# Attention's division moved behind the transpose-free layout: numerators, sums and reciprocals carried through DRAM by SyncE

## The chip, the core and the metric

The kernel runs on one core of a Trainium2 chip. The metric is the device time of one execution in microseconds (us); the kernel before takes 2135.75 us (median of three runs). A core has TensorE (PE: matmuls and transposes, called turns here), VectorE (DVE), ScalarE (ACT), GpSimd (POOL), and SyncE (SP), which here issues every DMA. SP takes its instructions in order: while it waits for a semaphore, nothing behind it is issued. The DMAs that it issues go to one queue, served by the core's 16 DMA engines.

## The reference, cut to what matters

A post-norm transformer layer on x of shape (32, 512, 256), with 16 heads of 16 features and a gated FFN of 768 hidden features, all in float32.

```python
qkv = x @ Wqkv
logits = jnp.einsum('bihd,bjhd->bhij', q, k) * scale
logits = logits + SLOPES[None, :, None, None] * rel[None, None, :, :]
logits = jnp.where(causal[None, None, :, :], logits, -jnp.inf)
attn = jax.nn.softmax(logits, axis=-1)
out = jnp.einsum('bhij,bjhd->bihd', attn, v).reshape(Bc, Tc, Dc)
...
x = _layernorm(x + out @ Wout)
gate = jnp.einsum('bsd,hd->bsh', x, wg)
up = jnp.einsum('bsd,hd->bsh', x, wu)
x = _layernorm(x + jnp.einsum('bsh,dh->bsd', silu(gate) * up, wd))
```

The change concerns the division inside the softmax: probabilities are left unnormalised, multiplied with v and a column of ones, and the result is divided by its own sum.

## The kernel before

The work is cut into units: batch b has two units, u = 2b and 2b + 1, of eight heads each; g = 0 or 1 names the group of four heads inside a unit. `Plan` writes one global order of steps, and every engine runs its own steps in that order. The plan goes through windows w. A window has two stages, `attention(w)` and `rest(w)`.

The attention stage interleaves, by the table `ATTENTION`, ten `first` tiles of unit w (PE) each with a `row_max` (DVE), ten `scores` tiles of unit w - 1 (PE) each with an `exp` (ACT) and a `select` (POOL), and three or four pieces of `pv` (PE), each group ending in `pv_copy` (ACT), which puts 128 rows of transposed numerators and sums into `pv_t[g]`: (w-2, 1) in the middle of the stage, (w-1, 0) later in it.

The rest stage has the other matmuls. It differs by part = w % 2. With part 0 (an even window) come `values`, turns of x1 and x, six `gate_up` tiles, `project(w+2, 0)`, `down`, `project(w+2, 1)`. With part 1 (an odd window) come `project(w+2, 0)`, turns of attn, six `gate_up` tiles, two halves of `project_out` (step "out"), `down` and `project(w+2, 1)`. Every `gate_up` tile is followed by `tanh` (ACT) and `silu` (two DVE operations), and `split_h` (`h_hi` on ACT, then `h_lo` on POOL), one tile behind. `down` needs the `split_h` of all six tiles, the last one for its last piece only.

Division before: `turn(u, g)` on PE turns `pv_t[g]` with four 128x128 transposes (L498) into PSUM, where tokens are the partitions. `divide` on DVE takes a reciprocal of the 16 sums (L821) and multiplies (L830) into `attn`. In the odd window PE turns `attn` back with eight transposes; `attn_hi` (ACT, L704) and `attn_lo` (DVE, L786) split it for the `out` matmuls.

SP before, in one window: `spread` (four DMAs of 256 KB, L460, SBUF to the DRAM buffer `bounce`), `gather` (eight DMAs, 1.5 MB, L471, from `bounce` to `q_rows` and `k_rows` of unit w + 1; needed by the first tile `first` of the next attention stage), in even windows `load_residual` and `load_x` (512 KB each, L451 and L444), `store_max` (four DMAs of 8 KB, L480; needed by the first `scores` of the next attention stage), and the output of `norm2` (L485).

## Time and profile before

| | |
|---|---|
| median of three runs | 2135.75 us (2134.16 to 2137.19) |
| the profiled execution | 2136.29 us, its span 2134.6 us |
| PE busy | 93% |
| DVE busy | 75% |
| ACT, POOL busy | 57%, 43% |
| granted TensorE clock, mean | 0.981 |
| DMA queue of SP | 48.5% of 16 engines, 226 MB |
| steady windows 1009.62 to 1040.69 and 1040.69 to 1072.85 | 31.07 and 32.16 us |

A busy share is an average over all stages; matmuls are pipelined, so a busy PE is not at its peak. A time such as 1024.12 is in us from the start of the span. R below is the start of a rest stage on PE: 1024.12 in an odd window and 1055.19 in an even one. An "idle before" or an arrow in a row names what ended the wait.

### The profile page before, as it was taken

What the parts mean: (1) busy time and instruction counts of PE and PEld (TensorE: products, weight loads), DVE (VectorE), ACT (ScalarE), POOL (GpSimd) and SP (SyncE); (2) the same over time, 40 slices, a digit from 0 to 9 for tenths busy, and PEclk for the clock granted to TensorE, in tenths of its full rate; (3) what the DMA queues carried; (4) which work ended last, traced back from release to release, by engine and by line L of the source; (5) the groups of instructions that cost most, each with busy time, mean ns of one, the idle gap of its engine ahead of it and who ended that gap; (6) DMA issues with size and microseconds to landing.
All of it is one profiled execution on the core that took longest, in us unless ns stands there. A gap on an engine that the chain in (4) does not pass through costs nothing.

```text
span 2134.6 us, 47883 instructions
## 1 busy us (share of the span) xinstructions
PE 1983.0 (93%) x19236; PEld 1550.0 (73%) x19236; DVE 1595.1 (75%) x2765; ACT 1223.5 (57%) x1999; POOL 928.5 (43%) x1924
## 2 busy tenths in 40 slices
PE   4779999999999999999999999999999999999986
PEld 3557777777777777777777777777877877777766
DVE  4557777787777787777778777778777778777754
ACT  1446656555655656655655665565565665566552
POOL 0123444444444453444454444444344445444444
PEclk8789999999999999999999999999999999999998
DMA  7455455355555445545545545545554544553500
GB/s 205 103 120 105 101 112 118 96 112 114 115 112 110 103 108 106 128 103 108 113 100 112 121 109 111 116 97 114 106 122 109 106 109 102 111 125 91 100 16 21
DMA packets 148830, 229.09 MB, mean 107 GB/s; under 512 B 13552, under 2 KB 64496, under 8 KB 148592
## 3 DMA queue, kind: packets, MB, share of 16 engines
q1 hardware_dynamic: 148608, 226.02, 48.5%
q8 instruction: 152, 2.49, 0.5%
q14 instruction: 70, 0.57, 0.1%
HBM read 139.98 MB, written 84.93 MB: 105 GB/s over the span
## 4 chain that ended last, share of the span: by engine, by line
PE 80%; DVE 10%; ACT 5%; DMA 2%; issue 1%; SPq 1%; POOL 0%; POOLq 0%; DVEq 0%
PE pair L495 72%; PE pair L498 8%; DVE row_max L801 7%; ACT probs L726 3%; DVE staged_lo L786 2%; ACT staged_hi L704 2%; DMA q_rows<-max_lo 1%; SPq L471 0%; DMA q_rows<-bounce 0%; DMA probs<-L_attn_Wout 0%; SPq L480 0%; DMA bounce<-staged_lo 0%; DVE row_max L803 0%; DVE xt_lo L786 0%; DVE x1t_lo L786 0%
## 5 line engine op out<-in xcount | busy, mean ns | idle before, releaser
L726 ACT ACTIVATE probs<-pair 128x1024 f32<-128x1024 f32 x640 | 627.1, 1027 | 150.1 <-PE pair L495 149.8
L903 POOL TENSOR_SCALAR_AFFINE_SELECT probs<-probs 128x256 f32<-128x256 f32 (+1 forms) x896 | 371.5, 440 | 445.9 <-ACT probs L726 445.1
L910 POOL TENSOR_TENSOR h_lo<-h_full,h_hi 128x256 fp32r<-128x256 f32 x384 | 283.2, 738 | 507.6 <-ACT h_hi L751 496.9
L803 DVE TENSOR_REDUCE row_max<-pair 128x8 f32<-128x1024 f32 x256 | 312.6, 1221 | 115.2 <-PE pair L495 114.7
L801 DVE TENSOR_REDUCE row_max<-pair 128x2 f32<-128x1024 f32 x256 | 311.9, 1218 | 71.2 <-PE pair L495 71.2
L495 PE MATMUL pair<-q_rows,k_rows 64*128 64x512 f32 (+3 forms) x2048 | 321.0, 370 | 38.4 <-DMA q_rows<-max_lo 20.8
L495 PE MATMUL pair<-k_rows,q_rows 52*128 52x512 f32 (+3 forms) x2048 | 299.6, 351 | 60.2 <-DVE staged_lo L786 26.1
L495 PE MATMUL pair<-probs,v_ones 128*32 128x512 f32 (+3 forms) x4096 | 319.3, 441 | 0.8 <-ACT probs L726 0.8
L495 PEld LDWEIGHTS pair<-q_rows,k_rows 64*128 64x128 f32 x2048 | 167.8, 188 | 157.2 <-ACT probs L726 92.2
L495 PEld LDWEIGHTS pair<-k_rows,q_rows 52*128 52x128 f32 x2048 | 179.0, 190 | 122.9 <-DVE row_max L801 62.9
L704 ACT ACTIVATE staged_hi<-pair 128x512 fp32r<-128x512 f32 x128 | 76.6, 599 | 269.9 <-PE pair L495 260.5
L743 ACT ACTIVATE h_full<-pair 128x256 f32<-128x256 f32 x384 | 144.6, 377 | 127.0 <-PE pair L495 126.2
L751 ACT ACTIVATE h_hi<-h_full 128x256 fp32r<-128x256 f32 x384 | 159.6, 416 | 86.4 <-DVE h_full L859 77.7
L495 PEld LDWEIGHTS pair<-probs,v_ones 128*32 128x32 f32 x4096 | 114.3, 110 | 128.5 <-issue 90.5
L495 PE MATMUL pair<-stair,turned 64*128 64x128 bf16 (+1 forms) x2560 | 175.2, 214 | 0.0
L859 DVE SCALAR_TENSOR_TENSOR h_full<-h_full,pair 128x256 f32<-128x256 f32 x384 | 161.7, 421 | 13.2
L734 ACT ACTIVATE pv_t<-pair 128x512 f32<-128x512 f32 x128 | 76.5, 598 | 159.4 <-PE pair L495 159.4
L495 PE MATMUL pair<-x1t_hi,wgate_t 128*128 128x256 f32 x768 | 162.6, 293 | 3.7 <-DVE x1t_lo L786 3.7
L855 DVE SCALAR_TENSOR_TENSOR h_full<-h_full,pair 128x256 f32<-128x256 f32 x384 | 158.2, 412 | 7.3 <-ACT h_full L743 6.1
L495 PE MATMUL pair<-wdown_t,h_hi 128*128 128x256 f32 x768 | 154.8, 283 | 0.6 <-POOL h_lo L910 0.6
L798 DVE TENSOR_REDUCE row_max<-pair 128x4 f32<-128x1024 f32 x128 | 155.4, 1214 | 0.0
L495 PE MATMUL pair<-x1t_hi,wup_t 128*128 128x256 f32 x768 | 155.1, 283 | 0.0
(88 smaller groups left out, 3622.7 us busy)
## 6 DMA issues: line engine op xcount, KB each, us to landing
bounce<-staged_hi SPq DMA_DIRECT2D x128, 256.0 KB
bounce<-staged_lo SPq DMA_DIRECT2D x128, 256.0 KB
q_rows<-bounce SPq DMA_DIRECT2D x128, 256.0 KB, 5.2
k_rows<-bounce SPq DMA_DIRECT2D x128, 256.0 KB, 6.2
x_sb<-L_attn_x SPq DMA_DIRECT2D x32, 512.0 KB, 10.4
k_rows<-bounce SPq DMA_DIRECT2D x128, 128.0 KB, 5.5
q_rows<-bounce SPq DMA_DIRECT2D x128, 128.0 KB, 6.7
x<-L_attn_x SPq DMA_DIRECT2D x32, 512.0 KB, 9.1
```

Source lines behind the costliest of these rows:

```text
L495: return tensor.matmul(o, lhs, rhs, start=start, stop=stop, skip_group_check=True, **kw)
L498: return tensor.transpose(o, i, ident[0:i.shape[0], 0:i.shape[0]])
L726: scalar.activation(probs[g][:, tile, :, :], pair[:, :, :], ACT.Exp, scale=scale).then_inc(s_exp, 1)
L743: scalar.activation(h_full[i % H_BUFFERS][:, :], bank[:, 0:half_tokens], ACT.Tanh, scale=0.5 * W_SCALE).then_inc(s_tanh, 1)
L751: scalar.activation(h_hi[:, m, :], h_full[(n_split_h[step] - 1) % H_BUFFERS][:, :], ACT.Copy).then_inc(s_h_hi, 1)
L798: vector.tensor_reduce(maxima[:, QB1, :, 2 * g:2 * g + 2], pair[:, :, :].rearrange("p s (a n) -> p s a n", a=2), AX.X, ALU.max).then_inc(s ...
L801: vector.tensor_reduce(maxima[:, QB3, :, p], pair[:, :, :], AX.X, ALU.max).then_inc(s_row_max, 1)
L803: vector.tensor_reduce(maxima[:, QB2_PARTS:QB0 + 1, :, p].rearrange("p b s -> p s b"), pair[:, :, :].rearrange("p s (b n) -> p s b n", n=P ...
L855: vector.scalar_tensor_tensor(h_full[z][:, :], h_full[z][:, :], 1.0, bank[:, 0:half_tokens], ALU.add, ALU.mult).then_inc(s_silu_half, 1)
L859: vector.scalar_tensor_tensor(h_full[z][:, :], h_full[z][:, :], 0.5 * W_SCALE * W_SCALE, bank[:, half_tokens:2 * half_tokens], ALU.mult, A ...
L903: made = pool.affine_select(out=diagonal, in_=diagonal, compare_op=ALU.is_ge, fill=0.0, base=0, pattern=[[0, diagonal.shape[1]], [1, P]], ...
L910: pool.tensor_tensor(h_lo[:, m, :], h_full[(n_split_h[step] - 1) % H_BUFFERS][:, :], h_hi[:, m, :].bitcast(F32), ALU.subtract).then_inc(s_ ...
```

## The change

- `turn` and the turns of attn are taken away from PE: 4 transposes for each (u, g), and 8 for each batch. The two-operation `divide` on DVE and `attn_lo` on DVE go with them.
- `send(u, g)`: SP writes `pv_t[g]` (128 rows of 512) to the DRAM buffer `pv_bounce`, after `pv_copy`.
- `fetch(u, g)`: SP waits for the send to land, then issues two DMAs: the numerators (64 rows, read in DRAM as 4 heads x 16 features x 512) into `attn[z]`, and the sums (4 heads x 512, laid over 128 partitions with 16 each) into `sums`.
- `recip(u, g)`: DVE takes the reciprocal of these 16 columns. `send_recip`: SP writes them to `recip_bounce` (DRAM).
- `fetch_recip(u, g)`: SP waits for that to land and reads 4 rows, each repeated 16 times, into 64 rows of `recips[z]`.
- `divide(u)`: one DVE multiply of 128x512 in SBUF. `attn_hi` on ACT and `attn_lo` on POOL follow, also 128x512.
- Places: `send` and `fetch` for (w-2, 1), and `send` for (w-1, 0), stand in the attention stage; `recip` and `send_recip` for (w-2, 1) at its end. In the rest stage SP has half of the gather, `fetch_recip(w-2, 1)`, the other half, `store_max`, `fetch(w-1, 0)`, the two loads, `send_recip(w-1, 0)`, the output, the spread, `fetch_recip(w-1, 0)`. `divide(w-2)` stands behind `gate_up` tile 3, `recip(w-1, 0)` behind tile 4. Both halves of `project_out` stand behind tile 5.

```diff
@@ attention(w)
                     self.add("pv_copy", u, g)
+                    self.add("send", u, g)
+                    if g == 1:
+                        self.add("fetch", u, g)
                     held = None
         self.norms()
+        if self.has(w - 2):
+            self.add("recip", w - 2, 1)
+            self.add("send_recip", w - 2, 1)
         if self.has(w):
             self.add("combine", w)
@@ rest(w)
         if self.has(w + 1):
-            self.add("gather", w + 1)
+            self.add("gather", w + 1, 0)
+        if self.has(w - 2):
+            self.add("fetch_recip", w - 2, 1)
+        if self.has(w + 1):
+            self.add("gather", w + 1, 1)
...
+        if has_ffn:
+            self.gate_up(ffn, part, range(0, 2))
+        self.max_row(w)
+        if self.has(w - 1):
+            self.add("fetch", w - 1, 0)
+        if part == 0:
             if 0 <= k - 1 < self.batches:
                 self.add("load_residual", k - 1)
...
+        if has_ffn:
+            self.gate_up(ffn, part, range(2, 4))
+        if self.has(w - 2):
+            self.add("divide", w - 2)
+        if has_ffn:
+            self.gate_up(ffn, part, range(4, 5))
+        if self.has(w - 2):
+            self.add("attn_hi", w - 2)
+            self.add("attn_lo", w - 2)
+        if self.has(w - 1):
+            self.add("recip", w - 1, 0)
+            self.add("send_recip", w - 1, 0)
+        if has_ffn:
+            self.gate_up(ffn, part, range(5, 6))
...
+        self.project(w + 2, 1)
+        if self.has(w - 1):
+            self.add("fetch_recip", w - 1, 0)
@@ SyncE
+                elif kind == "send":
+                    e.wait_ge(s_pv_copy, n_pv_copy["pv_copy", u, g])
...
+                    sync.dma_start(pv_bounce[z, g].rearrange("h c d t -> (h c d) t"), pv_t[g][:, :]).then_inc(s_sent[z][g], 16)
+                elif kind == "fetch":
+                    e.wait_ge(s_sent[z][g], (u // 2 + 1) * 16)
...
+                    sync.dma_start(attn[z][g * HALF:(g + 1) * HALF, :], pv_bounce[z, g, :, 0, :, :]).then_inc(s_fetched[z][g], 16)
+                    sync.dma_start(sums[z][:, g, :],
+                                   pv_bounce[z, g, :, 1, 0, :].rearrange("h (a n) -> h a n", n=sums[z].shape[2])).then_inc(s_fetched[z][g], 16)
+                elif kind == "fetch_recip":
+                    e.wait_ge(s_recip_sent[z][g], (u // 2 + 1) * 16)
...
+                    wide = bass.AP(tensor=r.tensor, offset=r.offset, ap=[list(r.ap[0]), [0, HEAD_DIM], list(r.ap[1])])
+                    sync.dma_start(recips[z][g * HALF:(g + 1) * HALF, :], wide).then_inc(s_recip_fetched[z][g], 16)
@@ VectorE
+                elif kind == "recip":
+                    e.wait_ge(s_fetched[z][g], (u // 2 + 1) * 16 * 2)
...
+                    vector.reciprocal(small_recips[z][:, g, :], sums[z][:, g, :]).then_inc(s_recip, 1)
                 elif kind == "divide":
-                    vector.reciprocal(rden[g][:, :, :], halves[:, :, :, HEAD_DIM]).then_inc(s_rden, 1)
...
-                    vector.tensor_tensor(o, halves[:, :, :, 0:HEAD_DIM], wide, ALU.mult).then_inc(s_divide, 1)
+                    for g in range(2):
+                        e.wait_ge(s_fetched[z][g], (u // 2 + 1) * 16 * 2)
+                        e.wait_ge(s_recip_fetched[z][g], (u // 2 + 1) * 16)
+                    vector.tensor_tensor(attn[z][:, :], attn[z][:, :], recips[z][:, :], ALU.mult).then_inc(s_divide, 1)
```

The order on SP at the end of an attention stage and in the even rest stage that follows. Before:

```order
L471 DMA q_rows<-bounce 32x4x512 [waits s_scores,s_bounced1]
L471 DMA k_rows<-bounce 16x4x512
L471 DMA k_rows<-bounce 32x4x512
...
L451 DMA x_0<-L_attn_x 128x4x256 [waits s_residual2]
L444 DMA x_sb<-L_attn_x 128x4x256 [waits s_work]
L480 DMA q_rows<-max_hi 1x4x512 [waits s_lo,s_hi]
```

And now, from the send of (w-2, 1) on:

```order
L502 DMA pv_bounce<-pv_t 128x512 [waits s_fetched01,s_pv_copy]
L510 DMA attn<-pv_bounce 64x1x512 [waits s_sent01]
L511 DMA sums<-pv_bounce 128x1x16
...
L519 DMA recip_bounce<-small_recips 128x16 [waits s_recip_fetched01,s_recip]
L485 DMA q_rows<-bounce 32x4x512 [waits s_scores,s_bounced1]
...
L529 DMA recips<-recip_bounce 64x1x512 [waits s_recip_sent01]
...
L494 DMA q_rows<-max_hi 1x4x512 [waits s_lo,s_hi]
...
L510 DMA attn<-pv_bounce 64x1x512 [waits s_attn_lo,s_sent10]
L511 DMA sums<-pv_bounce 128x1x16
L466 DMA x_0<-L_attn_x 128x4x256 [waits s_residual2]
L459 DMA x_sb<-L_attn_x 128x4x256 [waits s_work]
L519 DMA recip_bounce<-small_recips 128x16 [waits s_recip_fetched10,s_recip]
```

A `send_recip` that waits for DVE now stands ahead of the gather, `fetch_recip` stands inside it, and the two DMAs of `fetch(w-1, 0)` stand behind all of it and behind the maxima.

The order on DVE in an odd rest stage. Before, with both reciprocals near its start and reading PSUM:

```order
L810 TENSOR_REDUCE row_max<-row_max 128x8 [waits s_row_max]
L821 RECIPROCAL rden<-pair 128x16 [waits s_divide,s_work]
L830 TENSOR_TENSOR attn<-pair,rden 128x4x64 [waits s_rden]
L786 TENSOR_TENSOR staged_lo<-pair,staged_hi 128x512 [waits s_hi]
```

And now, the first line being the end of the attention stage:

```order
L861 RECIPROCAL small_recips<-sums 128x16 [waits s_recip_sent11,s_fetched11]
L852 TENSOR_REDUCE row_max<-row_max 128x8 [waits s_row_max]
L828 TENSOR_TENSOR staged_lo<-pair,staged_hi 128x512 [waits s_hi]
...
L869 TENSOR_TENSOR attn<-attn,recips 128x512 [waits s_recip_fetched11,s_recip_fetched10]
L894 SCALAR_TENSOR_TENSOR h_full<-h_full,pair 128x256 [waits s_tanh]
L898 SCALAR_TENSOR_TENSOR h_full<-h_full,pair 128x256 [waits s_silu_half]
L861 RECIPROCAL small_recips<-sums 128x16 [waits s_recip_sent00,s_fetched00]
L894 SCALAR_TENSOR_TENSOR h_full<-h_full,pair 128x256 [waits s_tanh]
```

DVE's three steps of the division now wait for DMAs (`s_fetched`, `s_recip_fetched`), and the last two tiles of `silu` (L894, L898) stand behind two of them.

## Rows read from the trace of the kernel before

**Rows 1.** The page: busy us, share of the span, instructions.

```profile
PE 1983.0 (93%) x19236; PEld 1550.0 (73%) x19236; DVE 1595.1 (75%) x2765; ACT 1223.5 (57%) x1999; POOL 928.5 (43%) x1924
```

**Rows 2.** Timeline of PE: start, us, operation; an odd and an even window.

```profile
1024.12 0.66 PE L498 MATMUL pair<-ident,pv_t 128*128 128x128 f32 x4
...
1026.02 0.60 PE L498 MATMUL pair<-ident,pv_t 128*128 128x128 f32 x4
1026.46 1.04 PE L498 MATMUL pair<-ident,attn 128*128 128x128 f32 x8
1027.25 0.48 PE L495 MATMUL pair<-x1t_hi,wgate_t 128*128 128x256 f32 x2
...
1036.37 0.41 PE L495 MATMUL pair<-wdown_t,h_hi 128*128 128x256 f32 x2
...
1040.69 0.50 PE L495 MATMUL pair<-q_rows,k_rows 64*128 64x512 f32 x2
...
1055.19 0.50 PE L495 MATMUL pair<-wqkv_hi,xt_hi 128*128 128x256 f32 x2
...
1072.85 0.50 PE L495 MATMUL pair<-q_rows,k_rows 64*128 64x512 f32 x2
```

**Rows 3.** Windows of the trace: busy by engine, PEclk, DMA share, GB/s.

```profile
1014.60:1020.60 6.00, 5.41 (x76) 3.05 (x78) 5.11 (x5) 4.27 (x5) 2.24 (x6) 1.00 0.51 165
1020.60:1021.60 1.00, 1.00 (x21) 0.44 (x17) 0.73 (x1) 0.00 (x0) 0.33 (x1) 1.00 0.12 45
1026.60:1034.60 8.00, 8.00 (x71) 7.92 (x69) 7.39 (x19) 4.74 (x12) 2.09 (x3) 1.00 1.07 164
1066.70:1069.70 3.00, 3.00 (x21) 2.73 (x21) 2.34 (x7) 2.41 (x7) 2.21 (x3) 1.00 1.04 311
```

**Rows 4.** Packets in 1009 to 1073, two windows long.

```profile
DMA packets 4552, 6.99 MB, mean 109 GB/s; under 512 B 416, under 2 KB 1952, under 8 KB 4544
```

**Rows 5.** SP's issues, and the PE row that waited for one of them.

```profile
87.56 1.19 SPq L480 DMA_DIRECT2D q_rows<-max_lo  x2
```

```profile
93.66 0.80 PE L495 MATMUL pair<-q_rows,k_rows 64*128 64x512 f32 x2 [8.84 <-DMA q_rows<-max_lo]
```

```profile
1024.21 0.60 SPq L471 DMA_DIRECT2D q_rows<-bounce  x1
...
1055.29 0.60 SPq L471 DMA_DIRECT2D q_rows<-bounce  x1
```

**Rows 6.** DMAs, us from issue to landing: gathers issued 85.45, 1028.68, 1059.76; an output.

```profile
q_rows<-bounce SPq DMA_DIRECT2D x1, 128.0 KB, 7.9
```

```profile
q_rows<-bounce SPq DMA_DIRECT2D x1, 128.0 KB, 8.3
```

```profile
q_rows<-bounce SPq DMA_DIRECT2D x1, 128.0 KB, 8.0
```

```profile
out<-result SPq DMA_DIRECT2D x1, 256.0 KB, 2.2
```

**Rows 7.** Timeline of DVE in the odd window.

```profile
1023.98 1.21 DVE L798 TENSOR_REDUCE row_max<-pair 128x4 f32<-128x1024 f32 x1
...
1035.76 0.42 DVE L855 SCALAR_TENSOR_TENSOR h_full<-h_full,pair 128x256 f32<-128x256 f32 x1
...
1036.57 0.69 DVE L839 TENSOR_TENSOR x<-pair,x 128x512 f32<-128x512 f32 x1
...
1038.08 0.25 DVE L847 BATCH_NORM_AGGREGATE moments<-stats 128x2 f32<-128x6 f32 x2
1039.41 0.69 DVE L870 SCALAR_TENSOR_TENSOR result<-pair,x 128x512 f32<-128x512 f32 x1 [1.09 <-PE pair L495]
...
1042.04 1.22 DVE L801 TENSOR_REDUCE row_max<-pair 128x2 f32<-128x1024 f32 x1
```

**Rows 8.** The page's groups: operation, busy, mean ns, idle before.

```profile
L910 POOL TENSOR_TENSOR h_lo<-h_full,h_hi 128x256 fp32r<-128x256 f32 x384 | 283.2, 738 | 507.6 <-ACT h_hi L751 496.9
...
L751 ACT ACTIVATE h_hi<-h_full 128x256 fp32r<-128x256 f32 x384 | 159.6, 416 | 86.4 <-DVE h_full L859 77.7
```

**Rows 9.** A window right after PE's 8.84 us wait, columns as in Rows 3.

```profile
93.70:98.20 4.50, 4.50 (x32) 2.77 (x36) 3.02 (x3) 3.07 (x3) 1.34 (x4) 0.50 0.43 165
```

More of the change, by code:

```diff
@@ L168, in project, with values @@
                 self.add("spread", u)
[L170 to L178 removed]
+    def values(self, b, t0):
+        self.take("values", b, t0)
+        self.add("values_out", b, t0)
     def max_row(self, u):
@@ L295, in build @@
     order = plan.order
-    n_work = tally(order, "x", "attn", "x1", "project", "values", "max_row", "turn", "out", "gate_up", "down", "weight")
+    n_work = tally(order, "x", "x1", "project", "values", "max_row", "out", "gate_up", "down", "weight")
     n_first, n_row_max, n_combine = tally(order, "first"), tally(order, "row_max"), tally(order, "combine")
@@ L299, in build @@
     n_hi, n_lo = tally(order, "split_hi"), tally(order, "split_lo")
-    n_values, n_pv_copy, n_divide = tally(order, "values_out"), tally(order, "pv_copy"), tally(order, "divide")
+    n_values, n_pv_copy = tally(order, "values_out"), tally(order, "pv_copy")
+    n_recip, n_divide, n_attn_hi, n_attn_lo = tally(order, "recip"), tally(order, "divide"), tally(order, "attn_hi"), tally(order, "attn_lo")
     n_tanh, n_silu, n_split_h = tally(order, "tanh"), tally(order, "silu"), tally(order, "split_h")
@@ L390, in build @@
             "x": lambda n, c: (P, xt_hi[:, c, :], xt_lo[:, c, :]),
-            "attn": lambda n, c: (P, attn_hi[:, c, :], attn_lo[:, c, :]),
             "x1": lambda n, c: (P, x1t_hi[:, c, :], x1t_lo[:, c, :]),
@@ L517, in _ @@
                         source = x_sb
-                    elif kind == "attn":
-                        e.wait_ge(s_divide, n_divide["divide", 2 * n + 1, 1])
-                        source = attn[n % 2]
                     else:
@@ L697, in _ @@
                         e.wait_ge(s_bounced[(i - 1) % 2], ((i - 1) // 2 + 1) * 16 * 4)
-                    if what == "attn" and i >= 1:
-                        e.wait_ge(s_work, n_work["out", i - 1, 2])
                     if what == "x1" and i >= 1:
```

166 lines of the change are left out of this document (81 added, 85 removed).

## The prediction, made before the changed kernel ran

> **What bounds the kernel now.** The page first: PE is busy 93% of the span [rows 1]. Then the timeline of PE over an odd and an even window [rows 2]: each has an attention stage of 14.5 us (1040.69 to 1055.19) and a rest stage, 16.57 us in the odd window (1024.12 to 1040.69) and 17.66 us in the even one (1055.19 to 1072.85). In the rest stages PE has no gap, so what is taken from PE there is gained, as long as nothing else is late. Then the transfers, since the change puts them in the path. The gather of 1.5 MB keeps all 16 DMA engines full (share 1.07, 164 GB/s), the spread of 1 MB only half of them (0.51, 165 GB/s), and it drains at about 1020.7 [rows 3], which is 11.1 us into its stage.
>
> **What is removed.** Twelve turns take from 1026.02 to 1027.25, 1.23 us [rows 2], 0.10 us each. A batch has 24 of them (four for each of four groups, eight for attn): 2.5 us. All 768 make 79 us, all on the path. DVE loses some 2 us a window, of which a reciprocal and a multiply come back; it has slack in the rest stages, so I count nothing for it.
>
> **Two facts about the queue.** First, a small transfer lands behind the bulk ahead of it. In the first windows the last two 8 KB maxima are issued at 87.56 to 88.75, and PE gets going with them at 93.66 [rows 5], while the gather's last part, issued at 85.45, lands 7.9 us later, at 93.35 [rows 6]. With an empty queue a 256 KB output needs 2.2 us from issue to landing [rows 6]. So the maxima waited for the gather and landed 0.3 us behind it.
>
> Second, how many engines serve a DMA. The 416 packets under 512 B in two windows [rows 4] are not data, since no transfer there has such short rows. They are one completion for each engine that takes part: 16 gathers, two outputs and two loads on 16 engines (320), eight spread DMAs on eight (64), eight maxima on four (32) give exactly 416. The spread's DMAs have an outermost dimension of 8, the maxima's source one of 4 rows. The new fetches read 4 heads x 16 x 512, 4 x 32 x 16 and 4 x 16 x 512: I take them to run on four engines. The Trainium skill says the same ("DMA: Bandwidth & Descriptors", section "Why a DMA increments its semaphore by 16 and not by 1"): the count of engines is the largest one up to 16 that divides both sides' slowest dimension. That is the rule that speaks against this change, and by it the outcome is that of my sum, not the second rival's.
>
> **Prices of the new transfers.** The spread moves 165 GB/s on eight engines, 20.6 GB/s each; 128 KB on four engines then takes 1.6 us. The nearest row on the other side is the gather, 164 GB/s on sixteen, 10.3 GB/s each: 3.2 us. I take 1.6, since the gather writes 16 or 32 partitions at a time and the fetch 64. The lower bound, on all engines, is 0.4. The sums are 32 packets of 64 B for each of four engines: not below 0 and, by the loads' 1 KB packets at 311 GB/s (53 ns each) [rows 3], not above 1.7 us; I take 0.8. The send, 256 KB, takes 0.8 of the output's 2.2 us (an estimate at 311 GB/s); 1.4 us is issue and landing, the landing about 0.4 of it.
>
> **When the gather can start.** In the attention stage, counted from its start: the spread drains at 11.1; `fetch_recip(w-2, 0)`, issued behind it, 1.6 more; `send(w-2, 1)` 0.8, landed at 13.9. SP waits for that, and then `fetch(w-2, 1)` needs 1.4 + 1.6 + 0.8, so that it lands at 17.7, which is R + 3.2 (R is the start of the rest stage). DVE would be ready for `recip(w-2, 1)` at R + 1.07 (1023.98 + 1.21) [rows 7], so it stands still, with `combine` behind it, and PE's turns of the maxima behind that. `send_recip` and its issue end at R + 4.1. Behind it in SP's order stands the gather, which started at R + 0.1 [rows 5]. It is 4 us late.
>
> **When it is over.** Gather G to last landing took 12.8 us in the odd window (1028.68 + 8.3 less 1024.21) and 12.5 in the even one (1059.76 + 8.0 less 1055.29) [rows 5, 6]. `fetch_recip(w-2, 1)` inside it adds 1.6, the maxima 0.3, the two DMAs of `fetch(w-1, 0)` 1.6 + 0.8. They land at R + 4.1 + 17.1 = R + 21.2 (odd), R + 20.9 (even). DVE wants them for `recip(w-1, 0)` behind the fifth tile, long before. Behind that recip on DVE stand the last `silu`, and in the odd window both `residual1`.
>
> - Even window: 20.9, recip 0.3, silu 0.85, `h_hi` 0.45, `h_lo` 0.8 [rows 7, 8], the last piece of `down` 0.5, project 1.45 (estimates from PE's timeline): 25.25 against 17.66, 7.6 us more.
> - Odd window: here DVE ends last. 21.2, recip 0.3, silu 0.85, two `residual1` of 1.7 each, `residual2` 1.75, `staged_lo` 0.7 to the first `row_max` of the next stage: 28.1. Before, that `row_max` started at 1042.04 [rows 7], R + 17.92. So 10.2 us more. The wait for `divide`, about R + 13.5 (half the gather and `fetch_recip`), and `attn_lo` on POOL behind it (twice the 0.74 of `h_lo` [rows 8]) keep PE from `out` until about R + 16.5; that lies inside the same sum.
>
> The 2.5 us of turns is already in these sums, since PE no longer sets the end. The two give 17.8 us a batch. PE now stands still for some 9 us in each window. After the 8.84 us wait of [rows 9] the granted clock is 0.50, the lower level of 1.2 GHz, for 4.5 us. In the even window that falls on the end of the stage and the start of the next: 2 us (half of 4.5, rounded down); in the odd window DVE covers it. 19.8 us a batch. Thirty batches run with all parts: 594. The first and last windows have the same round trips without the FFN: 30, an estimate. 2136.3 (the profiled execution, span plus 1.7; the median is 2135.75, the same) + 624 = **2760 us**.
>
> Other costs are nothing beside these: SP issues ten more DMAs a window at 0.6 us each [rows 5], hidden behind the drained or draining queue; if it were not, 6 us a window would be the outer bound, which the range holds.
>
> **Rivals.**
>
> 1. The fetches queue behind the gather, but on all 16 engines (0.4 and 0.2 us). Then `fetch(w-2, 1)` lands at R + 0.2, DVE isn't kept, the gather starts at R + 1.95, and `fetch(w-1, 0)` lands at about R + 16. That is 5.15 us less in each window: 7.5 a batch, with 1 for the clock 8.5, 255 and 15 for the ends: **2406 us**. For it: nothing but that the fetch's SBUF side has 64 rows. Against: the count of 416.
> 2. The fetches run at the gather's pace on four engines (3.2 and 1.5 us). The start of the gather moves by 3.9 and the end of the chain by 3.9 more, 15.6 a batch; with 3 for the clock 36.4, thirty times and 40: **3270 us**. For it: both read DRAM and write SBUF. Against: the fetch spreads over more partitions.
> 3. Not slower: small transfers pass the bulk and land in time. The point is `fetch(w-1, 0)`: it decides from about R + 9, where DVE comes to its recip. Then the 79 us come in: 2057 us. But `divide` behind tile 3, `attn_hi` and `attn_lo` (0.7 + 0.6 + 1.5) end near R + 10.2, and PE is at `out` at R + 7.7 (1036.37 less 1027.25 [rows 2], less 2.9 for both halves of `out`, plus 1.5 for the project, an estimate). That stall of 2.4 us an odd window gives back 72: **2129 us**, and with slightly less than that it is faster by a hair. Against: the maxima of [rows 5] did not pass.
>
> **How the numbers follow.** A difference of 0.2% (4.3 us) is about what a measurement can tell here. Forecast (2550 to 3000) 0.58; rival 1 0.20; rival 2 0.15; rival 3 0.07, of which 0.05 faster and 0.02 the same. The predicted time is the forecast's. The range, 2400 to 3150, holds the forecast, rival 1 and a part of rival 2; about 2 in 10 is left out. Slower 0.93.
>
> **What would show it.** In the changed profile: DVE waits for a DMA into `sums` at both recips, the one in the rest stage by over 5 us, and longer than the one at the stage's start; `sums` and `attn` take over 10 us from issue to landing in the rest stage and about 4 in the attention stage; the first gather of a window is issued some 4 us after R; PE waits before `out` and before `down`'s last piece, and PEclk shows stretches of 0.5; the small packets per window grow as four for each fetch. Wrong would be: DVE waits under 1 us at `recip(w-1, 0)` (rival 3), a gather start at R + 2 with fetches that take under 1 us behind the gather (rival 1), or DMA engines busy without a gap through the whole window (rival 2). My weakest numbers are the 1.6 and the 0.8.

## The result, and the profile of the changed kernel

The changed kernel takes **2921.15 us** (median, 2919.03 to 2923.26) against 2136.47 for the kernel before, measured beside it: 1.367 times as long, 95% interval 1.3651 to 1.3698. The forecast was 2760 with a range of 2400 to 3150. The direction, the mechanism and the range held; the sum was 161 us short. PE does the same matmuls less the turns, and is busy 71% of the span where it was 93% [rows 1]. Its busy time is longer all the same, 2085 us for 18468 instructions where 19236 took 1983: the mean granted clock of the profiled execution is 0.85, where it was 0.98. From the page of the changed kernel (busy us by engine, small packets, the chain by engine and by line):

```profile
PE 2085.2 (71%) x18468; PEld 1609.8 (55%) x18468; DVE 1539.0 (53%) x2637; ACT 1218.8 (42%) x1999; POOL 1008.0 (35%) x1988
PEclk8788878888889888888898888888898888888887
...
DMA packets 220000, 298.28 MB, mean 102 GB/s; under 512 B 51952, under 2 KB 102896, under 8 KB 219760
...
DMA 41%; PE 22%; SPq 16%; DVE 9%; ACT 5%; POOL 3%; issue 3%; POOLq 0%; DVEq 0%
```

The chain that ended last is now DMA and SP's queue for 57% of the time, and the granted clock (PEclk, tenths) is mostly 8. The list of waits says who stands still for what (total us, times, longest), and for SP's own queue:

```profile
DVE small_recips L861 <- DMA sums<-pv_bounce: 603.5, 125, 12.2
...
DVE attn L869 <- DMA recips<-recip_bounce: 342.8, 63, 9.8
PE pair L543 <- POOL attn_lo L955: 327.0, 32, 14.1
...
PE pair L543 <- POOL h_lo L949: 296.6, 62, 7.4
```

```profile
SPq L519 <- DVE small_recips L861: 733.1, 127, 10.5
...
SPq L510 <- DMA pv_bounce<-pv_t: 308.5, 64, 6.1
```

These sums must not be added: they overlap, and the experiments show that to take one away uncovers another.

One even window, read in order. Its attention stage starts at 1411.38 and its rest stage, R, at 1425.88. SP's queue (start, us taken to issue, operation), which answers to [rows 5]:

```profile
1416.99 1.31 SPq L475 DMA_DIRECT2D bounce<-staged_lo  x1
1418.40 1.35 SPq L529 DMA_DIRECT2D recips<-recip_bounce  x1
1419.86 1.29 SPq L502 DMA_DIRECT2D pv_bounce<-pv_t  x1
1426.52 0.55 SPq L510 DMA_DIRECT2D attn<-pv_bounce  x1
1427.12 0.52 SPq L511 DMA_DIRECT2D sums<-pv_bounce  x1
...
1431.24 0.33 SPq L519 DMA_DIRECT2D recip_bounce<-small_recips  x1
1431.66 0.62 SPq L485 DMA_DIRECT2D q_rows<-bounce  x1
...
1437.49 0.61 SPq L485 DMA_DIRECT2D q_rows<-bounce  x1
...
1441.49 0.55 SPq L511 DMA_DIRECT2D sums<-pv_bounce  x1
1442.09 0.48 SPq L466 DMA_DIRECT2D x<-L_attn_x  x1
1442.61 0.56 SPq L459 DMA_DIRECT2D x_sb<-L_attn_x  x1
```

The send issued at 1419.86 is landed by 1426.5, only then can the fetch be issued, and the gather starts at 1431.66, R + 5.8, where it had started at R + 0.1. DVE, in the same window (brackets: idle before, and what ended it), answering to [rows 7]:

```profile
1430.96 0.25 DVE L861 RECIPROCAL small_recips<-sums 128x16 f32<-128x16 f32 x1 [4.01 <-DMA sums<-pv_bounce]
...
1443.57 0.69 DVE L869 TENSOR_TENSOR attn<-attn,recips 128x512 f32<-128x512 f32 x1 [3.63 <-DMA recips<-recip_bounce]
...
1451.93 0.25 DVE L861 RECIPROCAL small_recips<-sums 128x16 f32<-128x16 f32 x1 [6.88 <-DMA sums<-pv_bounce]
```

and PE, which had no gap in this stage before [rows 2]:

```profile
1447.00 0.50 PE L543 MATMUL pair<-wdown_t,h_hi 128*128 128x256 f32 x2 [3.19 <-POOL h_lo L949]
1454.22 0.80 PE L543 MATMUL pair<-wdown_t,h_hi 128*128 128x256 f32 x2 [6.43 <-POOL h_lo L949]
```

The odd window that follows (R = 1472.40) has the division at 1488.08 after 7.12 us of waiting, PE in front of `out` until 1490.92, and the second reciprocal at 1494.54:

```profile
1488.08 0.69 DVE L869 TENSOR_TENSOR attn<-attn,recips 128x512 f32<-128x512 f32 x1 [7.12 <-DMA recips<-recip_bounce]
...
1494.54 0.25 DVE L861 RECIPROCAL small_recips<-sums 128x16 f32<-128x16 f32 x1 [4.98 <-DMA sums<-pv_bounce]
```

```profile
1490.92 0.77 PE L543 MATMUL pair<-wout_hi,attn_hi 128*128 128x256 f32 x2 [10.12 <-POOL attn_lo L955]
```

Windows of this even stage (us, busy by engine, PEclk, DMA share, GB/s), answering to [rows 3] and [rows 9]:

```profile
1440.00:1447.00 7.00, 3.81 (x27) 3.34 (x25) 1.45 (x3) 2.08 (x5) 2.95 (x4) 1.00 1.08 116
1447.00:1452.00 5.00, 0.78 (x4) 0.53 (x4) 0.07 (x1) 0.00 (x0) 0.00 (x0) 0.55 0.92 157
1452.00:1458.00 6.00, 3.78 (x12) 2.79 (x12) 3.17 (x9) 0.42 (x1) 1.22 (x4) 0.52 0.10 32
```

From 1447 to 1452 hardly any engine computes while the DMA engines are busy for 92% of the time, and then PE works at a granted clock of 0.52, its lower level of 1.2 GHz, while the DMA engines are busy for 10%.

The packets of this even and the odd window (1411.38 to 1500.17), answering to [rows 4]:

```profile
DMA packets 6775, 9.14 MB, mean 103 GB/s; under 512 B 1616, under 2 KB 3152, under 8 KB 6768
```

**One table for all kernels.** DVE's and SP's rows give every window the same four marks. A window is counted from the first `row_max` on DVE to the next first one; E is the end of the last `row_max` of the stage (1.07 us behind R); G the issue of the first gather DMA; then the start of the second reciprocal, `recip(w-1, 0)`, and of `divide`. Medians over the windows between 600 and 1800 us, 12 to 19 of each kind (which windows count at the edges moves a median by 0.1); even / odd:

| kernel | us | window | E to G | G to divide | G to second recip |
|---|---|---|---|---|---|
| before | 2136 | 32.2 / 31.1 | -1.0 / -1.0 | | |
| changed | 2921 | 46.1 / 42.7 | 4.6 / 3.4 | 11.3 / 11.5 | 20.0 / 17.8 |
| free_recip | 2660 | 39.2 / 41.8 | 0.9 / 0.6 | 14.6 / 13.0 | (waits for nothing) |
| free_divide | 2544 | 39.4 / 36.3 | 2.1 / 1.3 | (no transfer) | 15.5 / 14.3 |
| split16 | 2603 | 39.1 / 39.2 | 2.5 / 1.4 | 9.3 / 9.4 | 15.0 / 14.8 |
| loads_late | 2863 | 44.0 / 42.7 | 4.7 / 3.4 | 11.4 / 11.4 | 17.8 / 17.9 |
| two_mends | 2582 | 39.1 / 38.8 | 2.6 / 1.5 | 9.2 / 9.4 | 14.9 / 14.8 |
| act_ring | 3029 | 47.0 / 44.9 | 4.6 / 3.3 | 11.5 / 13.9 | 21.0 / 15.3 |
| three_mends | 2607 | 37.4 / 40.5 | 2.7 / 1.1 | 9.8 / 11.3 | 13.5 / 12.7 |
| one_trip_early | 2423 | 36.8 / 35.9 | -0.9 / -1.0 | | |
| one_trip_cover | 2406 | 35.5 / 36.1 | -0.9 / -0.9 | | |
| one_trip_no_recip | 2156 | 31.9 / 30.8 | -1.0 / -1.0 | | |
| one_trip_quarters | 2406 | 36.3 / 35.7 | -1.0 / -1.0 | | |
| no_transfers | 2188 | 32.5 / 32.1 | -1.0 / -1.0 | | |

The attention stage itself is 14.2 us of `row_max` in every kernel. So the loss is wholly in the rest stages: 13.9 us in the even and 11.6 in the odd ones.

### The profile page after: what moved, and what is told of

Read it like the earlier page. It is cut to its first block, busy times and chain, and to the rows that moved or that the text cites. A ratio compares the mean times of both kernels' runs of the same rounds, so it can differ in the third digit from the quotient of the medians.

```text
span 2921.5 us, 47506 instructions
## 1 busy us (share of the span) xinstructions
PE 2085.2 (71%) x18468; PEld 1609.8 (55%) x18468; DVE 1539.0 (53%) x2637; ACT 1218.8 (42%) x1999; POOL 1008.0 (35%) x1988
## 4 chain that ended last, share of the span: by engine, by line
DMA 41%; PE 22%; SPq 16%; DVE 9%; ACT 5%; POOL 3%; issue 3%; POOLq 0%; DVEq 0%
PE pair L543 22%; DMA sums<-pv_bounce 22%; DMA pv_bounce<-pv_t 12%; SPq L485 7%; DMA recips<-recip_bounce 6%; SPq L494 3%; SPq L510 2%; DVE row_max L843 2%; ACT probs L761 2%; SPq L475 2%; SPq L529 1%; POOL attn_lo L955 1%; DVE staged_lo L828 1%; ACT pv_t L769 1%; DVE small_recips L861 1%
## 5 line engine op out<-in xcount | busy, mean ns | idle before, releaser
L543 PE MATMUL pair<-wdown_t,h_hi 128*128 128x256 f32 x768 | 177.0, 314 | 296.6 <-POOL h_lo L949 296.6
L543 PE MATMUL pair<-q_rows,k_rows 64*128 64x512 f32 (+3 forms) x2048 | 328.8, 378 | 41.3 <-DMA q_rows<-max_lo 23.1
L861 DVE RECIPROCAL small_recips<-sums 128x16 f32<-128x16 f32 x128 | 32.4, 253 | 603.5 <-DMA sums<-pv_bounce 603.5
L543 PE MATMUL pair<-wout_hi,attn_hi 128*128 128x256 f32 x256 | 82.1, 420 | 327.0 <-POOL attn_lo L955 327.0
L543 PEld LDWEIGHTS pair<-wdown_t,h_hi 128*128 128x128 f32 x768 | 131.4, 207 | 314.6 <-POOL h_lo L949 311.9
L543 PEld LDWEIGHTS pair<-wout_hi,attn_hi 128*128 128x128 f32 x256 | 65.8, 314 | 332.6 <-issue 329.1
L869 DVE TENSOR_TENSOR attn<-attn,recips 128x512 f32<-128x512 f32 x64 | 45.0, 703 | 342.8 <-DMA recips<-recip_bounce 342.8
L543 PE MATMUL pair<-x1t_hi,wgate_t 128*128 128x256 f32 x768 | 168.7, 302 | 58.4 <-DVE x1t_lo L828 58.4
L955 POOL TENSOR_TENSOR attn_lo<-attn,attn_hi 128x512 fp32r<-128x512 f32 x64 | 80.9, 1263 | 362.9 <-ACT attn_hi L776 362.8
L776 ACT ACTIVATE attn_hi<-attn 128x512 fp32r<-128x512 f32 x64 | 40.3, 630 | 363.7 <-DVE attn L869 363.7
```

The lines of the kernel that those rows point to most:

```text
L543: return tensor.matmul(o, lhs, rhs, start=start, stop=stop, skip_group_check=True, **kw)
L955: pool.tensor_tensor(attn_lo[:, u % 2, :], attn[u % 2][:, :], attn_hi[:, u % 2, :].bitcast(F32), ALU.subtract).then_inc(s_attn_lo, 1)
```

## The experiments

Twelve kernels, each an edit of the changed kernel or of another of them. Those given without an interval were timed once. The kernel before was timed seven times beside each four, and lay within 0.2% of its median; of the changed kernel and its variants that were timed four times, all lay within 0.4% but one_trip_no_recip, whose runs lie 1.1% apart. So a difference of some 20 us between two kernels that were timed once is a weak one.

**1. The transfers left out.** Numerators and sums are multiplied straight from SBUF; the division and all DMAs of it are gone. What stays is the order of the matmuls without turns.

```diff
-                    self.add("send", u, g)
-                    if g == 1:
-                        self.add("fetch", u, g)
...
-            self.add("recip", w - 2, 1)
-            self.add("send_recip", w - 2, 1)
...
-                    for g in range(2):
-                        e.wait_ge(s_fetched[z][g], (u // 2 + 1) * 16 * 2)
-                        e.wait_ge(s_recip_fetched[z][g], (u // 2 + 1) * 16)
-                    vector.tensor_tensor(attn[z][:, :], attn[z][:, :], recips[z][:, :], ALU.mult)
+                    vector.tensor_tensor(attn[z][:, :], pv_t[z][0][:, :], pv_t[z][1][:, :], ALU.mult)
```

> The changed kernel without any of its new transfers: no send, fetch, reciprocal or its two DMAs. The multiply reads the two pv_t buffers of its unit (doubled, so that nothing waits for them), so the division by the sums is left out. Everything else (no turns, attn_hi on ACT, attn_lo on POOL, the order) stands as in the changed kernel. Theory A (the loss is DVE, ACT, POOL and PE waiting for small transfers that land behind the bulk): 2129 us, the 79 us of turns won and some 70 of them lost to PE's wait for attn_lo before out. Theory C (the new order, or POOL's attn_lo, costs by itself): still over 2250 us.

Measured: 2187.77 us, 1.0235 times before (1.0218 to 1.0252). So 733 of the 785 us are the transfers and what waits for them. The time lies between the two theories, 59 us above theory A. But even without one transfer the kernel is 51 us slower than before, though 79 us of turns are gone. PE's timeline shows why, in an even and an odd window:

```profile
1017.76 0.48 PE L491 MATMUL pair<-x1t_hi,wgate_t 128*128 128x256 f32 x2 [0.84 <-DVE x1t_lo L776]
```

```profile
1054.89 0.47 PE L491 MATMUL pair<-wout_hi,attn_hi 128*128 128x256 f32 x2 [2.57 <-POOL attn_lo L895]
```

The turns had been work for PE while ACT and DVE split x1; without them `gate_up` waits 0.84 us. The split of attn, at its new place and on POOL, keeps `out` waiting 2.57 us (the third rival had said 2.4). The removed work was also cover: for the 0.84 us experiment 10 puts this to the test.

**2. The sums not waited for.** `sums` holds ones, and the DMA into it is left out; the reciprocals wait for nothing.

```diff
-                    sync.dma_start(sums[z][:, g, :],
-                                   pv_bounce[z, g, :, 1, 0, :].rearrange("h (a n) -> h a n", n=sums[z].shape[2])).then_inc(s_fetched[z][g], 16)
```

> The changed kernel with the DMA into sums left out; the reciprocal takes a constant tile of ones and waits for no DMA. All other transfers, 128 KB and 256 KB ones, stay. The division by the sums is left out. Theory A: the gather starts about 2 us into the rest stage again, the even window falls back to about its old length, in the odd one PE still waits for attn_lo until about 14.6 us into the stage: 2300 us. Theory B (throughput: the added bytes keep the DMA engines or DRAM busy, whoever waits): nearly all bytes are still moved, so over 2750 us.

Measured: 2659.77 us, between the two. A wait of 603 us was taken away and 261 came back. The even window falls by 6.9 us, the odd one by 0.9 only, and the division is still waited for. From its list of waits:

```profile
DVE attn L870 <- DMA recips<-recip_bounce: 395.9, 63, 9.9
```

In the odd window two chains end side by side: the second reciprocal with DVE's work behind it, and the division with `attn_hi`, `attn_lo` and PE's `out`, `down` and project behind it. With one gone the other sets the same end. This is read from the marks of the windows; experiment 3, which frees the other chain, brings the sums sooner as well, so it does not separate the two cleanly.

**3. The division not waited for.** The other half: `fetch_recip` is left out and `recips` holds ones.

```diff
-            self.add("fetch_recip", w - 2, 1)
...
-            self.add("fetch_recip", w - 1, 0)
...
-                        e.wait_ge(s_recip_fetched[z][g], (u // 2 + 1) * 16)
```

> The other half of free_recip, on the changed kernel: fetch_recip is left out and the division multiplies by ones as soon as the numerators are there; the sums still come through DRAM, the reciprocals are still taken and sent ahead of the gather. Theory P (two chains end side by side in the odd window, and the reciprocal's chain sets the even one; what is gained is the four-engine transfers of fetch_recip, ahead of the send and in the gather, some 3.5 us a window): 2670-2730 us. Theory L (the 343 us of waits for the rows stand in the path by themselves and add to the others): 2560-2600 us. If only the waits counted and the four-engine transfers cost nothing: 2880-2921 us.

Measured: 2543.85 us, below all that was expected, and nearer theory L; 377 us for a wait of 343. Nothing waits for the rows now, but the wait for the sums is shorter too:

```profile
DVE small_recips L850 <- DMA sums<-pv_bounce: 521.6, 120, 12.0
```

The table shows where: without `fetch_recip(w-2, 0)` ahead of the send the gather starts 2.5 / 2.1 us sooner, and without `fetch_recip(w-2, 1)` inside the gather the sums land 4.5 / 3.5 us sooner behind G. So one `fetch_recip` of 128 KB costs what stands behind it 2.1 to 2.5 us, and 3.5 to 4.5 inside the gather. The forecast had 1.6. The two savings make 7.0 us in the even and 5.6 in the odd window, of the 6.7 and 6.5 by which the windows fall. So it is the mechanism of theory P, at 5.6 to 7.0 us a window in place of 3.5, that gives nearly theory L's number.

**4. Fetches on 16 engines.** Each fetch of 64 rows is cut into four of 16 rows.

```diff
-                    sync.dma_start(attn[z][g * HALF:(g + 1) * HALF, :], pv_bounce[z, g, :, 0, :, :]).then_inc(s_fetched[z][g], 16)
+                    for h in range(GROUP):
+                        r0 = g * HALF + h * HEAD_DIM
+                        sync.dma_start(attn[z][r0:r0 + HEAD_DIM, :], pv_bounce[z, g, h, 0, :, :]).then_inc(s_fetched[z][g], 16)
```

(`fetch_recip` in the same way.)

> Each fetch of attn and each fetch_recip is cut into four DMAs of 16 rows, which by the count of small packets should run on 16 engines instead of 4; same bytes, same order, six more DMA issues of 0.55 us for each group. The sums stay on four engines. If the four engines are part of the cost: 1.2 us less for each of four such pieces a window, less the later issue of some 1.6 us in the attention stage: about 2730 us. If the number of engines has no part: the longer issue alone, 2921 to 2980 us.

Measured: 2603.47 us, 318 less, for 12 more DMAs to issue in each window. The small packets of two windows (1257.3 to 1335.0) show that the edit does what it is meant to: 2096 where the changed kernel has 1616. The 480 more are eight fetches with four completions each that have become 32 DMAs with 16 each.

```profile
DMA packets 7255, 9.14 MB, mean 118 GB/s; under 512 B 2096, under 2 KB 3632, under 8 KB 7248
```

The pages of the changed kernel and of this one (KB each, median us from issue to landing) show it on DMAs that only stand behind a fetch:

```profile
pv_bounce<-pv_t SPq DMA_DIRECT2D x128, 256.0 KB, 4.1
x_sb<-L_attn_x SPq DMA_DIRECT2D x32, 512.0 KB, 12.0
```

```profile
pv_bounce<-pv_t SPq DMA_DIRECT2D x128, 256.0 KB, 2.3
x_sb<-L_attn_x SPq DMA_DIRECT2D x32, 512.0 KB, 5.0
```

The send, which stands behind `fetch_recip`, now takes what an output takes [rows 6]. Counted from the start of the stage it is even issued 2.3 / 1.1 us later, and the fetch that waits for it is still issued 1.8 / 1.7 us sooner. The loads, behind the numerators and sums, take 7 us less from issue to landing. Not all of that is the engines: split16 issues `load_x` 13.7 us behind G (median) where it was 10.5, when more of the gather has drained, so that counted from G it lands some 4 us sooner. (In the kernel before, with no fetch on four engines ahead of it, it is issued 5.8 us behind G and takes 10.4.) The reading that fits both is that a transfer served by four engines keeps these four busy, and what stands behind it and uses all sixteen waits for them. In the table G comes 2.1 / 2.0 us sooner and the sums 4.9 / 3.0 sooner behind it; 12 us a batch less, somewhat over 10 of which reach the windows. What limits it now is another thing: in the chain that ended last SP's own issuing has 40% of the time, where it had 16%.

```profile
SPq 40%; DMA 22%; PE 14%; DVE 9%; POOL 8%; issue 5%; ACT 2%; DVEq 0%; POOLq 0%
```

**5. The loads later.** `load_residual` and `load_x` stand behind `send_recip(w-1, 0)` in SP's order.

```diff
-        if part == 0:
-            if 0 <= k - 1 < self.batches:
-                self.add("load_residual", k - 1)
-            if 0 <= k + 1 < self.batches and k + 2 < self.batches:
-                self.add("load_x", k + 2)
...
             self.add("send_recip", w - 1, 0)
+        if part == 0:
+            if 0 <= k - 1 < self.batches:
+                self.add("load_residual", k - 1)
+            if 0 <= k + 1 < self.batches and k + 2 < self.batches:
+                self.add("load_x", k + 2)
```

> The two 512 KB loads of the even window move behind send_recip(w-1, 0) in SyncE's order, so that nothing of theirs is queued when the sums are awaited. If loads queued behind the fetch slow what stands ahead of them (the even window's fetch lands 20.2 us after the gather starts, the odd window's 17.7): 2.5 us in each batch or more, 2830 to 2850 us. If a queue's later transfers don't touch earlier ones: 2921 us.

Measured: 2862.54 us, 59 less, where 71 to 91 were expected. In the even window the sums land 2.2 us sooner behind G, in the odd one, which has no loads, nothing changes (17.8 and 17.9). So here a transfer queued *behind* another slowed it: the loads were issued 0.6 and 1.1 us after the sums' fetch and were queued for over 9 us of its way.

**6. The two together,** the edits of 4 and 5 and nothing else (two_mends). Its expectation speaks of three_mends, experiment 8, which ran before it.

> split16 and loads_late together, without ScalarE's queue. If ScalarE's queue cost three_mends 1.3 us in the odd windows (26.3 against 25.0 us of rest stage in split16) and the loads' place is what shortened its even ones (23.1 against 24.9): 31 times 1.8 us under split16, 2530-2560 us. If the shorter even windows came from ScalarE's queue and the loads' place gives nothing once 16 engines serve the fetches: 2590-2610 us.

Measured: 2581.95 us, between the two cases: 21 us under split16, where the loads' place had given 59 alone. The even window is not shorter than in split16; what is gained stands in the odd one (38.8 against 39.2), and why was not looked into. Once 16 engines serve the fetches, the loads' place shortens the even window no more.

**7. The fetch on another queue.** `fetch(w-1, 0)` is issued by ACT.

```diff
+                elif kind == "fetch" and key[1] == 0:
+                    u, g = key
...
+                    scalar.dma_start(attn[z][g * HALF:(g + 1) * HALF, :], pv_bounce[z, g, :, 0, :, :]).then_inc(s_fetched[z][g], 16)
```

> The two DMAs of fetch(w-1, 0) are issued by ScalarE, on a queue of their own, and no longer by SyncE behind the gather; nothing else changes. Theory Q (they land late because they stand in SyncE's queue behind the gather's descriptors): they land some 4 us after their issue, most of the rest stage's wait before the reciprocal goes (sums of 603 us of waits falls below 350), and the time falls to 2700-2780 us; not further, since with the reciprocal's wait wholly gone (free_recip) it was 2660. Theory E (they land late because the 16 DMA engines are full, in whichever queue they stand): still over 9 us from issue to landing, the waits for the sums stay over 550 us, and the time is within 30 us of 2921.

Measured: 3029.2 us, 108 *more*: neither theory. In an even window, SP starts the gather at 1485.22 and ACT issues the sums' fetch 4.2 us later, with three of the gather's eight DMAs not yet issued; DVE gets the sums at 1506.27:

```profile
1489.41 0.52 ACTq L779 DMA_DIRECT2D sums<-pv_bounce  x1
```

```profile
1506.27 0.25 DVE L871 RECIPROCAL small_recips<-sums 128x16 f32<-128x16 f32 x1 [8.10 <-DMA sums<-pv_bounce]
```

16.9 us from issue to use, where it was 10.4 (1441.49 to 1451.93). Counted from G the sums come no sooner in the even window, 21.0 against 20.0. In the odd one they come 2.5 us sooner (15.3 against 17.8), but the rows of `fetch_recip` 2.4 later (13.9 against 11.5), and the division is the chain that counts there. The second queue brought no second set of engines here: it let the fetch compete with what the order on one queue had kept ahead of it. The Trainium skill ("DMA: Bandwidth & Descriptors", section "Issuing engines are not separate DMA queues") says that DMAs started by different engines run on the same 16 DMA engines and interleave, and that only issue time is saved. The trace agrees, with the 16.9 us.

**8. All three,** the edits of 4, 5 and 7 (three_mends).

> Three edits of the changed kernel at once: fetches split so that 16 engines serve them, the loads behind the reciprocal's send, and fetch(w-1, 0) on ScalarE's queue. Both round trips stay. If the three causes add up, 2603 less 59 and less what the queue alone gives: 2400-2500 us. If the division's trip (reciprocal out, rows back, inside the gather) holds the window once the others are gone, 2540-2600 us. On neither theory does it come to the 2188 of the kernel without transfers, since send and reciprocal still stand ahead of the gather in SyncE's order.

Measured: 2606.9 us, no better than split16 alone and 7 us above the second theory's range. The even window is 1.7 us shorter than in split16, the odd one 1.3 longer, again through the rows of `fetch_recip` (G to division 11.3 against 9.4). The best of the mends that leave both round trips in the window came to 2582. Others were not tried: in two_mends too SP's issuing has 40% of the chain, and no run served the fetches with 16 engines without more DMAs to issue.

**9. One trip in place of two, used late.** The product with the column of ones leaves each sum 16 times over, so the fetch can bring them straight into 64 rows beside the numerators. The reciprocal is then taken on 128x512, and no second trip is needed. `fetch(w-1, 0)` gets a whole window to land.

```diff
-                    sync.dma_start(sums[z][:, g, :],
-                                   pv_bounce[z, g, :, 1, 0, :].rearrange("h (a n) -> h a n", n=sums[z].shape[2])).then_inc(s_fetched[z][g], 16)
+                    sync.dma_start(recips[z][g * HALF:(g + 1) * HALF, :], pv_bounce[z, g, :, 1, :, :]).then_inc(s_fetched[z][g], 16)
...
+                    vector.reciprocal(recips[z][:, :], recips[z][:, :]).then_inc(s_recip, 1)
+                    e.wait_ge(s_recip, n_divide[step])
                     vector.tensor_tensor(attn[z][:, :], attn[z][:, :], recips[z][:, :], ALU.mult).then_inc(s_divide, 1)
...
         self.max_row(w)
+        if self.has(w - 2):
+            self.add("divide", w - 2)
+            self.add("attn_hi", w - 2)
+            self.add("attn_lo", w - 2)
```

> One trip through DRAM in place of two: the fetch takes the numerators and the sums, which the values' product already holds sixteen times over, straight into the rows where the division wants them; VectorE takes the reciprocal of 128x512 there, and no reciprocal goes out or comes back. Division and split stand right behind the fold of the maxima, so that fetch(w-1, 0) has a whole window to land. Theory S (the cost is that DMAs which something waits for in the same window stand behind the bulk, and the second trip): 2188 of the kernel without transfers, less most of its 2.57 us wait before out in the odd windows (31 of them, 80 us at most), plus up to 1 us a window (62 us) for the later start of the gather and VectorE's reciprocal: 2110-2230 us. Theory T (any trip of the values through DRAM costs, by the engines' load): over 2350 us.

Measured: 2422.74 us, 1.1345 times before (1.1325 to 1.1365): 498 us better than the changed kernel, and above theory S by 193. The number lies in theory T's range (over 2350), but T's cause does not show: DVE waits for these DMAs 13 us in the whole run, the gather starts where it did before, and yet 286 us are missing.

**10. The same, with x1's turns moved.**

```diff
-            if 0 <= k < self.batches:
-                self.values(k, 0)
-                self.values(k, 2)
             if has_ffn:
                 self.transposed("x1", ffn)
+            if 0 <= k < self.batches:
+                self.values(k, 0)
+                self.values(k, 2)
```

> As one_trip_early, and in the even windows the transposes of x1 stand ahead of the values' products in place of behind them, so that ScalarE and VectorE split x1 while TensorE has other work, as the removed turns had let them. If the 0.84 us before gate_up in the kernel without transfers is this lost cover, the time falls by about 31 times 0.84 = 26 us against one_trip_early; if it is some other wait, by nothing.

Measured: 2405.92 us, 1.1263 times before (1.1244 to 1.1282), 17 less, where 26 were expected; PE's wait for `x1t_lo` in front of `gate_up` falls from 29.9 us in 32 places to 3.7 in two. The lost cover of experiment 1 is confirmed, at two thirds of its size. What remains is in DVE's rows of the odd window:

```profile
1212.37 3.33 DVE L830 RECIPROCAL recips<-recips 128x512 f32<-128x512 f32 x1
1215.73 0.69 DVE L832 TENSOR_TENSOR attn<-attn,recips 128x512 f32<-128x512 f32 x1
1217.39 0.42 DVE L857 SCALAR_TENSOR_TENSOR h_full<-h_full,pair 128x256 f32<-128x256 f32 x1 [0.97 <-ACT h_full L755]
```

```profile
1218.58 0.77 PE L513 MATMUL pair<-wout_hi,attn_hi 128*128 128x256 f32 x2 [3.95 <-POOL attn_lo L918]
```

A reciprocal of 512 columns takes 3.33 us, five times the multiply of the same size (0.69). The `silu` of four tiles stands behind it. The reciprocal of 16 columns takes 0.25: this is what the second trip had bought.

**11. That reciprocal left out.** The last kernel without it; attn is numerator times sum.

> As one_trip_cover, with VectorE's reciprocal of 128x512 left out, so that attn is numerator times sum and not divided. All transfers stay. Theory V (the reciprocal, 3.34 us in each of 64 windows with the silu of four tiles behind it, is what is left of the loss): the time falls by 64 times 3.34 = 214 us or more, to 2110-2195 us. Theory W (the transfers themselves, 256 KB out and 256 KB back four times a batch, still hold the windows): by under 80 us, over 2325.

Measured: 2156.34 us (2140.51 to 2163.43), 1.0096 times before (1.0075 to 1.0118), 250 us less than with it. Theory V, the reciprocal, holds, and more than its 214 us go. All bytes of numerators and sums still travel through DRAM, and a pair of windows takes 63.2 us in the mean, as before. The time lies between the kernel before (2136) and the one without any transfer (2188, without the moved turns and the early split). That does not make the bytes free: the kernel with these two moves and no transfer was not run. An estimate for it is 2188 less the 17 of experiment 10 and less 47 (PE's wait for `attn_lo` falls from 83.8 us there to 36.5), 2124 us, so that the transfers still cost some 32 us. The profile shows where: a wait for the maxima at the start of the scores in 43 windows, where before had five (20.8 us), and 14% of the chain that ended last.

```profile
PE pair L513 <- DMA q_rows<-max_lo: 58.2, 43, 9.5
```

The profiled execution is the fastest of the four (2140.51 us); what made the others up to 23 us longer is not shown.

**12. The reciprocal in quarters,** spread between the tiles of `gate_up`, `down` ahead of `out`.

```diff
+        for m in (2, 3, 4):
+            if has_ffn:
+                self.gate_up(ffn, part, range(m, m + 1))
+            if self.has(w - 2):
+                self.add("recip", w - 2, m - 1)
...
+                    part = recips[z][:, c * P:(c + 1) * P]
+                    vector.reciprocal(part, part).then_inc(s_recip, 1)
```

> As one_trip_cover, but VectorE's reciprocal is cut into four of 128x128, one behind the fold of the maxima and one behind each of the next three tiles of gate_up, division and split behind the last tile, and down ahead of out. VectorE's work is the same. If its place in the order was the cost (four tiles' silu stood behind 4 us), most of the 4 us a window comes back: 2200-2290 us. If VectorE is full in the rest stages, the order gains nothing: 2380-2430 us.

Measured: 2405.54 us, 1.1251 times before (1.1234 to 1.1268), the same as one_trip_cover. DVE is full: in an odd window it runs from 1217.58 to 1227.82 without a gap, a tile of `silu` and a quarter taking 1.6 us where PE needs 0.95 for a tile of `gate_up`, and then

```profile
1225.54 0.95 DVE L837 RECIPROCAL recips<-recips 128x128 f32<-128x128 f32 x1
1226.40 0.36 DVE L868 SCALAR_TENSOR_TENSOR h_full<-h_full,pair 128x256 f32<-128x256 f32 x1
1226.80 0.42 DVE L872 SCALAR_TENSOR_TENSOR h_full<-h_full,pair 128x256 f32<-128x256 f32 x1
1227.14 0.68 DVE L843 TENSOR_TENSOR attn<-attn,recips 128x512 f32<-128x512 f32 x1
1230.91 0.69 DVE L883 SCALAR_TENSOR_TENSOR result<-pair,x 128x512 f32<-128x512 f32 x1 [3.09 <-PE pair L519]
```

it waits for PE, which at 1229.65 has waited 1.50 us for the last `h_lo`. This order doesn't help. No version found here beats the kernel before, whose division on turned data needs 16 columns and no transfer.

## Why the prediction was right, and where it was short

- **The mechanism.** DVE waits for the sums at both reciprocals, longer at the one in the rest stage (6.88 against 4.01 even, 4.98 against 2.61 odd, "over 5" just missed in the odd one); from issue to use the sums take 10.4 / 8.3 us in the rest stage and 3.8 in the attention stage (forecast: over 10, missed in the odd one, and 4). PE waits in front of `out` and of `down`'s last piece. All places were as forecast.
- **Four engines.** The count of small packets decides it. Two windows had 416 [rows 4]; the same query over 1411.38 to 1500.17 now gives 1616. The 1200 more are 300 for each of four groups: 128 rows of sums, 128 rows of 64 B of reciprocals, 16 completions for each of the two sends, and four for each of three fetches. That is four engines exactly, and the rival with 16 engines falls; split16, which builds its condition for all but the sums, came to 2603 and not to its 2406. The rival at the gather's pace (3270) had the better price for `fetch_recip`, 3.2, and a far too high one for the other two. This count agrees with the rule that the prediction cites from the Trainium skill ("DMA: Bandwidth & Descriptors", section "Why a DMA increments its semaphore by 16 and not by 1"). The prediction says that the rule speaks against its second rival; it speaks against the first, since the second too has four engines.
- **The odd window** was forecast at +10.2 us and is +11.6. The second reciprocal was to start at R + 21.2 and started, in the median, 1.1 us later. The division came at R + 15.7 (forecast 13.5) and `out` at R + 18.5 (16.5): so the chain through `out`, which the forecast called covered, ends level with DVE's. Experiments 2 and 3 bear on it: without the first chain the odd window gains 0.9, without the second 6.5, of which 5.6 are that the sums come sooner.
- **The even window** was forecast at +9.6 with the clock and is +13.9. Here two terms failed. The gather's start was put at R + 4.1 and is R + 5.7 in the median: the send landed 15.0 us after the start of the attention stage, not 13.9, and the fetch behind it took 4.4 us, not 3.8. And from G to the sums it is 20.0 us, not 16.8. Of these 3.2, 2.2 are the loads (loads_late), which stand behind the fetch and for which the prediction has no term.
- **The prices.** The 1.6 us for a `fetch_recip` was too small, 2.1 to 2.5 ahead of the send and 3.5 to 4.5 inside the gather; the 2.4 for numerators and sums too large: in free_divide, odd window, G to the sums is 14.3, and gather and maxima alone were put at 13.1, which leaves 1.2. The two errors nearly cancel, which is why the odd sum came out. By its total alone this could not have been seen.
- **The clock** fell to 0.52 to 0.55 behind PE's waits, as [rows 9] had let expect. From 1454.22 to the stage's end at 1457.89 PE took 3.7 us for what was put at 1.95, so 1.7 against the forecast's 2 for that stretch and the start of the next stage.
- **The sum.** 13.9 + 11.6 = 25.5 us a batch against 19.8; thirty batches make 765, and the ends some 20. The 161 us missing are 5.7 us a batch, 4.3 of them in the even window, less 10 at the ends.
- **The third rival,** 2129 us if nothing came late, was 59 too low (no_transfers, 2188). It had the stall before `out` right (2.57 against 2.4) and took the whole 2.5 us of turns as won in every batch. In the even window nothing is won: `gate_up` waits 0.84 us for the split of x1 that the turns had covered, and the window is 0.3 us longer than before.

## What to carry to other kernels

When a result goes through DRAM and comes back in the same stage, count what stands ahead of it in the queue, on how many engines each DMA there runs, and also what is queued right behind it; then give it a window of its own (with one such trip, and the reciprocal left out, this kernel came to 2156 us, between the kernel before and the one without any transfer). Before a serial step of few columns is moved to full width, look at what the operation costs per column: a reciprocal is not a multiply. Work that is removed from a full engine may have been cover for another one, so a gain counts only as far as the next operation's inputs are ready.

## What the runs showed of the hardware

- A DVE reciprocal takes 0.25 us for 16 columns, 0.94 for 128 and 3.34 for 512, about 6.2 ns a column from the two longer ones; a multiply of 512 columns 0.69 us.
- A DMA on four engines slowed those behind it: a send of 256 KB needed 4.1 us from issue to landing behind one such, and 2.3 with the same bytes on 16 (medians). The loads needed 12.0 and 5.0, but some 3 us of these 7.0 are their later issue behind the gather.
- A later, larger DMA slowed an earlier one in the same queue (2.2 us in the even window), and a fetch issued on a second queue beside the gather took 16.9 us where it had taken 10.4 behind it.
- SP's issues took 1.3 us each, in place of 0.6, from the fourth DMA of the spread on (1416.99 to 1421.15). What holds them there was not looked into. Nor was it told apart why a `fetch_recip` costs more inside the gather than ahead of a send.
